# Attention, FFN and expert layers on one core: whole-array tail and B/C products, a masking in one pass, scales for each token tile apart, and a new order of the pieces

## The reference

```python
# sublayer 1: a chunked state-space mixer (64 heads of 8, state of 64)
B_mat = _rope_pairs(_rms_norm(B_mat) * B_norm_bias, cos, sin)     # 64 wide
C_mat = _rope_pairs(_rms_norm(C_mat) * C_norm_bias, cos, sin)
y = _ssd_chunked(x_gamma, A, B_mat, C_mat, dt) + _ssd_chunked(x_beta, A, B_shift, C_mat, dt)
# sublayer 2: a gated FFN, 704 hidden features, integer weights
gate = silu(x @ ((wq_gate - 128) * s_gate).T)
out = (gate * (x @ ((wq_up - 128) * s_up).T)) @ ((wq_down - 128) * s_down).T
# sublayer 3: attention by running sums, then a gated FFN of 1024
q, k, v = split(rms(x) @ w_qkv.T); q = rms(q); k = rms(k); w = exp(k)
y = sigmoid(q) * cumsum(w * v) / (cumsum(w) + 1e-6)
x = x + (u * silu(g)) @ w_out.T                       # u, g = split(y @ w_swiglu.T)
# sublayer 4: 16 experts of 448 hidden features, the best 4 of them for each token
```

## Time and profile before

| | us |
|---|---|
| median of 3 runs | 1955.8 (1946.88 to 1957.39) |
| the profiled execution | 1958.51 |
| its span, first to last instruction | 1956.7 |
| PE busy over the span | 1740.7 (89%) |
| DVE, POOL, ACT busy | 1320.4 (67%), 844.3 (43%), 751.6 (38%) |

### The profile page before, as it was taken

The page is one execution under the profiler, slowest core; times in us unless marked ns, Lnnn a source line. Parts: engine busy times, 40 slices in busy tenths (PEclk is TensorE's granted clock), DMA queues, the critical chain, the costliest instruction groups (busy, mean ns, idle before and its releaser), DMA issues. The chain is left out here.

```text
span 1956.7 us, 34760 instructions
## 1 busy us (share of the span) xinstructions
PE 1740.7 (89%) x8580; PEld 1208.8 (62%) x8581; DVE 1320.4 (67%) x3085; ACT 751.6 (38%) x1398; POOL 844.3 (43%) x791
## 2 busy tenths in 40 slices
PE   4699999999999999999999998863999999999980
PEld 2367667667677677676686675651655556665650
DVE  3788888888888888888889887321444444444435
ACT  3335445345345344454453452221322232332323
POOL 2033243333433433432533433123666667676654
PEclk7799999999999999999999999886999999999995
DMA  5523132142232231331321322636999999999997
GB/s 191 179 83 124 42 105 85 60 124 63 82 114 62 88 119 51 93 124 41 104 93 58 117 70 70 262 136 168 164 162 153 160 172 172 169 171 171 163 138 260
DMA packets 369673, 242.79 MB, mean 124 GB/s; under 512 B 250641, under 2 KB 348241, under 8 KB 369233
## 3 DMA queue, kind: packets, MB, share of 16 engines
q1 hardware_dynamic: 303824, 170.22, 32.6%
q0 software_dynamic: 40704, 67.40, 18.3%
q10 hardware_dynamic: 25088, 4.50, 1.2%
HBM read 121.33 MB, written 68.78 MB: 97 GB/s over the span
## 5 line engine op out<-in xcount | busy, mean ns | idle before, releaser
L1689 PE MATMUL pu<-w_all,xh 128*128 x1728 | 364.4, 357 | 56.1 <-DMA xh<-xin 40.6
L1689 PEld LDWEIGHTS pu<-w_all,xh 128*128 128x128 bf16 x1728 | 168.6, 99 | 209.3 <-issue 91.8
L1820 POOL DMA_INDIRECT sums_dram<-yo,meta_in x144 | 229.1, 1591 | 135.3 <-issue 70.9
L1772 DVE TENSOR_TENSOR hid<-pu,gate 128x448 f32<-128x448 f32 x144 | 90.0, 625 | 253.3 <-PE pu L1689 138.5
L838 PE MATMUL pb<-x1T,w_sw 128*128 128x256 f32 x1024 | 234.6, 384 | 0.7 <-ACT x1T L956 0.7
L838 PEld LDWEIGHTS pb<-x1T,w_sw 128*128 128x128 f32 x1024 | 193.3, 191 | 53.7 <-issue 14.9
L1704 PE MATMUL py<-w_all,hh 128*128 x1584 | 197.8, 274 | 3.0 <-DMA hh<-hs 3.0
L1704 PEld LDWEIGHTS py<-w_all,hh 128*128 128x128 bf16 x1584 | 155.7, 98 | 45.0 <-issue 4.2
L652 PE MATMUL pa<-w_in,xT 128*128 128x512 f32 (+1 forms) x384 | 159.8, 562 | 23.5 <-DVE masked L1272 14.2
L1807 POOL DMA_INDIRECT xin<-x_dram,meta_in x144 | 142.3, 988 | 67.7 <-issue 46.9
L1102 POOL DMA_INDIRECT xgs<-xg_dram,chosen_rows x112 | 122.1, 1091 | 93.0 <-DMA xg_dram<-xg 47.7
(11 more groups left out here) (244 smaller groups left out, 3118.4 us busy)
## 6 DMA issues: line engine op xcount, KB each, us to landing
w_stage<-in_w_ug SPq DMA_DIRECT2D x64, 224.0 KB
split_ug<-w_parts SPq DMA_DIRECT2D x64, 224.0 KB
w_all<-split_ug SPq DMA_DIRECT2D x16, 896.0 KB, 8.9
xg_dram<-xg SPq DMA_DIRECT2D x16, 512.0 KB, 2.8
w_stage<-in_w_dn SPq DMA_DIRECT2D x32, 256.0 KB
split_dn<-w_parts SPq DMA_DIRECT2D x32, 256.0 KB
w_all<-split_dn SPq DMA_DIRECT2D x16, 512.0 KB, 10.1
rows<-sums_dram SPq DMA_DIRECT2D x32, 256.0 KB, 5.3
```

Of the source, the lines that this page charges most:

```text
L1689: last = mm(pu[:, 2 * b + w, 0:EH], xh[:, m % XS, DC * xp + c, :], w_ug[:, bass.ds(e, 1), wp, c, w * EH:(w + 1) * EH], start=n == 0, stop= ...
L1820: nc.gpsimd.indirect_dma_start(out=sums_dram[m % 2], out_offset=bass.IndirectOffsetOnAxis(ap=meta[:, m, 0:1], axis=0), in_=yo[:, m % XS, : ...
```

## The change

- The 64 last gate columns and the 64 last up columns stand side by side in one weight (`w_gu`), so B1.5 is one product with 128 output rows (gate in rows 0 to 63, up in 64 to 127). ACT writes silu of the gate into partitions 64 to 127; the product with up goes into a tile of its own, `h_tail`, whose first 64 rows are zero, as are those of the last slice of `w_down`. B2.t then runs over 128 rows.
- `bcr` gets a third slot, with zeros ahead of B and C: the transposes of A3 are 128 wide, and A3L's products run over 128 rows, of which half are zeros or are multiplied by zeros.
- Masking: ACT copies the first tile's product to `cb_own`, DVE writes the second tile's over it under one mask, and one masked copy then fills `masked` for all levels.
- POOL makes the q/k scales for each token tile apart, ACT follows with that tile's k and q exponentials; B4.0 waits for the third of the four exponentials.
- `nothing` is half as wide and stored twice over by a repeated read; `sq_b` is gone (the squares are written into `yc`).
- Two pieces are cut in two (C7H from C7L, G1B from G1 on DVE), and the order of pieces is new on PE, ACT, POOL and DVE.

```diff
@@ ORDER
-    "PE": ("C7 A2 C7L F3.0 F3.1 B1T C8 A2L B1.0 B1.1 A3 B1.2 B1.3 B1.4 A3L B1.5 B2.0 B2.1 G1+ A4.0 B3T A4.1 B3.0 B3.1 "
-            "A4.2 B3V A4.3 A4.4 B4.0 B4.1 G2.0+ G2.1+ B5T A4.5 B5.0 B5.1 B5.2 A4.6 ...
+    "PE": ("C7 A2 C7L F3.0 F3.1 B1T A2L B1.0 C8 B1.1 A3 B1.2 B1.3 B1.4 A3L B1.5 B2.0 B2.1 A4.0 A4.1 G1+ B3T A4.2 B3.0 "
+            "B3.1 B3V A4.3 B4.0 G2.0+ B4.1 A4.4 G2.1+ B5T A4.5 B5.0 B5.1 A4.6 B5.2 ...
-    "ACT": ("A2 C7 WH.0 C7L A2S F3 B1T C8 A2L B1.0 B1.1 WH.1 A3 B1.2 B1.3 B1.4 A3L B1.5 G1+ B3T G2+ WH.2 B3 B3L B5T B5.0 "
-            "B5.1 G4+ B5.2 WH.3 WH.4 B5.3 B5.4 G3+ B5.5 B5.6 A5 B5.7 WH.5 A5L"),
-    "POOL": ("C7 A6- A2 AX.0 A2L AX.1 B2 B3 D8+ G1+ A5 B6"),
+    "ACT": ("A2 WH.0 C7 C7L A2S F3 WH.1 B1T C8 A2L B1.0 B1.1 B1.2 A3 WH.2 B1.3 B1.4 A3L B1.5 G1+ B3T WH.3 G2+ B3.0 B3.1 "
+            "B3L.0 B3L.1 G3+ B5T B5.0 B5.1 B5.2 B5.3 B5.4 B5.5 B5.6 WH.4 A5 B5.7 A5L WH.5 G4+"),
+    "POOL": ("C7 A6- A2 AX.0 AX.1 A2L B2 B3.0 B3.1 D8+ G1+ A5 B6"),
@@ PE: b1, b2, a3, b4
-                for w, weight in enumerate((w_gate, w_up)):
+                for w, first in enumerate((j * P, FM + j * P) if j < FJ - 1 else (2 * FM,)):
                     for c in range(DC):
-                        last = mm(pb[0:rows, 1 + j % 2, w * T:(w + 1) * T], weight[:, c, j * P:j * P + rows],
+                        last = mm(pb[:, 1 + j % 2, w * T:(w + 1) * T], w_gu[:, c, first:first + P],
...
-                    last = mm(pb[:, 3, t * D:(t + 1) * D], hT[0:rows, j, t * P:(t + 1) * P], w_down[0:rows, j, :],
-                              start=j == 0, stop=j == FJ - 1)
+                    h = hT[:, j, t * P:(t + 1) * P] if j < FJ - 1 else h_tail[:, t * P:(t + 1) * P]
+                    last = mm(pb[:, 3, t * D:(t + 1) * D], h, w_down[:, j, :], start=j == 0, stop=j == FJ - 1)
...
-                        last = nc.tensor.transpose(pa[0:N, 3, (2 * t + m) * P:(2 * t + m + 1) * P],
-                                                   bcr[:, t, m, :], ident)
+                        last = nc.tensor.transpose(pa[:, 3, (2 * t + m) * P:(2 * t + m + 1) * P],
+                                                   bcr[:, t, m:m + 2, :].rearrange("p z n -> p (z n)"), ident)
...
-                    pe.wait_ge(kq_exp.sem, kq_exp.at(s))
+                    pe.wait_ge(kq_exp.sem, kq_exp.at(s, 2 * NT - 1))
@@ DVE: a3_late
-                for t in range(NT):
-                    vec.copy_predicated(masked[:, :, :], halves[:, t, :, :], spread(pa[:, 2, t * P:(t + 1) * P], 1, LV)
-                                        ).then_inc(masked_ready.sem, 1)
...
+                vec.copy_predicated(cb_own[:, :], halves[:, LV, :], pa[:, 2, P:2 * P]).then_inc(masked_ready.sem, 1)
+                dve.wait_ge(masked_ready.sem, masked_ready.at(s, 1))
+                carrier.take()
+                vec.copy_predicated(masked[:, :, :], halves[:, 0:LV, :], spread(cb_own[:, :], 1, LV)
+                                    ).then_inc(masked_ready.sem, 1)
@@ POOL: b3, ACT: b3_late
+                pool.wait_ge(qk_ss_ready.sem, qk_ss_ready.at(s, 2 * (t + 1)))
+                root_mean(pb_, qk_ss[:, t, :], D, RMS_EPS).then_inc(qk_rms_ready.sem, 1)
...
+                act.wait_ge(qk_rms_ready.sem, qk_rms_ready.at(s, t + 1))
+                act_f(wv[:, t, 0, :], pb[:, 1 + t, D:2 * D], ACT.Exp, scale=qk_ss[:, t, 1:2]).then_inc(kq_exp.sem, 1)
+                act_f(eq[:, t, :], pb[:, 1 + t, 0:D], ACT.Exp, scale=qk_ss[:, t, 0:1]).then_inc(kq_exp.sem, 1)
```

More of the change, by code:

```diff
@@ L37 @@
 FJ = (FH + P - 1) // P
+FT = FH - (FJ - 1) * P
+FM = FH - FT
 SH = 1024
@@ L398, in layers_block @@
         padding = sb("padding", [P, cap // P, 4], U32)
-        nothing = sb("nothing", [P, NT * D])
+        nothing = sb("nothing", [P, D])
         w_stage = sb("w_stage", [P, 2, EJ // 2 * D])
@@ L937, in a3_late @@
                 act.wait_ge(cb_ready.sem, cb_ready.at(s))
+                act_f(cb_own[:, :], pa[:, 2, 0:P], ACT.Copy).then_inc(cb_copied.sem, 1)
                 act_f(cb_cross[:, :], pa[:, 3, 0:P], ACT.Copy).then_inc(cb_copied.sem, 1)
@@ L961, in b1 @@
             def b1(s, j):
-                rows = min(P, FH - j * P)
+                rows, to = (P, 0) if j < FJ - 1 else (FT, P - FT)
                 act.wait_ge(ffn_projected.sem, ffn_projected.at(s, j + 1))
@@ L965, in b1 @@
                     act.wait_ge(ffn_h.sem, ffn_h.at(s, j - 1))
-                act_f(sg[0:rows, j % 2, :], pb[0:rows, 1 + j % 2, 0:T], ACT.Silu,
+                act_f(sg[to:to + rows, j % 2, :], pb[0:rows, 1 + j % 2, 0:T], ACT.Silu,
                       scale=s_gu[0:rows, 0, j:j + 1]).then_inc(ffn_silu.sem, 1)
@@ L1077, in b2, with b3 @@
                                             ).then_inc(norm2[1].sem, 1)
-            def b3(s):
-                pb_.start(s)
-                pool.wait_ge(qk_ss_ready.sem, qk_ss_ready.at(s))
-                root_mean(pb_, qk_ss[:, :, :].rearrange("p t m -> p (t m)"), D, RMS_EPS).then_inc(qk_rms_ready.sem, 1)
-                pb_.end()
+            def b3(s, t):
+                if t == 0:
+                    pb_.start(s)
+                pool.wait_ge(qk_ss_ready.sem, qk_ss_ready.at(s, 2 * (t + 1)))
+                root_mean(pb_, qk_ss[:, t, :], D, RMS_EPS).then_inc(qk_rms_ready.sem, 1)
+                if t == NT - 1:
+                    pb_.end()
             def a2(s):
@@ L1382, in b1 @@
             def b1(s, j):
-                rows = min(P, FH - j * P)
                 dve.wait_ge(ffn_silu.sem, ffn_silu.at(s, j + 1))
-                vec.scalar_tensor_tensor(hT[0:rows, j, :], pb[0:rows, 1 + j % 2, T:2 * T], s_gu[0:rows, 1, j:j + 1],
-                                         sg[0:rows, j % 2, :], ALU.mult, ALU.mult).then_inc(ffn_h.sem, 1)
+                a = P - FT
+                if j == FJ - 1:
+                    vec.scalar_tensor_tensor(h_tail[a:P, :], pb[a:P, 1 + j % 2, 0:T], s_gu[a:P, 1, j:j + 1],
+                                             sg[a:P, j % 2, :], ALU.mult, ALU.mult).then_inc(ffn_h.sem, 1)
+                    return
+                vec.scalar_tensor_tensor(hT[:, j, :], pb[:, 1 + j % 2, T:2 * T], s_gu[:, 1, j:j + 1],
+                                         sg[:, j % 2, :], ALU.mult, ALU.mult).then_inc(ffn_h.sem, 1)
             def b2(s):
@@ L1410, in b2_second, with b3 @@
                 normalised_twice(s, 0, x2, x2_ready)
-            def b3(s):
-                dve.wait_ge(v_projected.sem, v_projected.at(s))
-                for t in range(NT):
-                    dve.wait_ge(kq_exp.sem, kq_exp.at(s, t + 1))
-                    vec.tensor_tensor(wv[:, t, 1, :], wv[:, t, 0, :], pb[:, 3, t * D:(t + 1) * D], ALU.mult
-                                      ).then_inc(wv_ready.sem, 1)
+            def b3(s, t):
+                if t == 0:
+                    dve.wait_ge(v_projected.sem, v_projected.at(s))
+                dve.wait_ge(kq_exp.sem, kq_exp.at(s, 2 * t + 1))
+                vec.tensor_tensor(wv[:, t, 1, :], wv[:, t, 0, :], pb[:, 3, t * D:(t + 1) * D], ALU.mult
+                                  ).then_inc(wv_ready.sem, 1)
             def b4(s, part):
@@ L1962, in host_arrays @@
     pad = FJ * P - FH
-    s_gu = np.stack([np.pad(a(f"L0_ffn_s_{n}"), (0, pad)).reshape(FJ, P).T for n in ("gate", "up")], 1)
+    s_gate = np.pad(a("L0_ffn_s_gate"), (0, pad))
+    s_up = a("L0_ffn_s_up")
+    s_up = np.concatenate([s_up[:FM], np.zeros(pad, s_up.dtype), s_up[FM:]])
+    s_gu = np.stack([s_gate.reshape(FJ, P).T, s_up.reshape(FJ, P).T], 1)
+    gate, up = a("L0_ffn_wq_gate").T, a("L0_ffn_wq_up").T
     down = a("L1_ffn_W_down").transpose(0, 2, 1)
```

97 lines of the change are left out of this document (46 added, 51 removed), and 10 rows, old and new, of the table ORDER.

## The result

| | before | changed |
|---|---|---|
| median of 6 runs, us | 1955.19 (1946.88 to 1957.39) | 1948.48 (1944.29 to 1950.33) |
| the profiled execution, us | 1958.51 | 1946.5 |
| its span, us | 1956.7 | 1944.7 |
| one round of the steady part, us | 75.70 | 75.2 |

The ratio is 0.9959, with a 95% interval of 0.994 to 0.9978: 0.4% faster, where 1.2% was forecast. The time lies inside the range; the size is a third of what was promised. A round gained 0.5 us and not 1.5.

A forecast was written before the change was run, and what follows sets the result against it. PE was taken as the bound, DVE nearly as tight before x2n. Per round -0.56 us up to B3T and -0.96 behind it, -1.5, times 16 = -24.3 us from 1958.5, less 2.7 for the median: 1932 us, range 1905 to 1950.

The forecast's parts named there:

- PE's own work: PE, each round: B1.5 loses 4 of 8 records (-0.86 us), array size changes go (-1.40 us); together -2.26 us.
- PE up to the down product: PE before B2.0: nothing gained before B1.0, B1.2 waits 0.1 us; B2.0 starts at about 722.0 instead of 723.12.
- The large copy and y: DVE's large masked copy starts at about 722.05 and ends at 723.3; POOL's y wants to start at 722.7, during it.
- the bounds of the hold: DVE before x2n: y beside the copy holds u 0.9 us, y behind it 1.4 us; 1.1 us taken.
- rival B: y gets in ahead of the large copy; PE stops 1.5 us in the down product; 1944 us, chance 0.14.
- The sentence on the Trainium skill: Shared DVE/POOL port pair locked by whichever starts first: the large copy keeps y out, hold 1.4 us, sum 5 us worse.
- the second bound: y starts behind the large copy at 723.3 and ends at 725.3, so u on DVE is held 1.4 us.
- Behind B3T: Rest of the round after B3T: A4.1 moved ahead -0.86 us, B4.0 waits 0.3 more, B5T's 0.4 wait goes; -0.96 us.
- x2n: PE's wait for x2n ahead of B3T is the longest of its waits, 1.5 to 2 us a round.
- A: Rival: the y product costs nothing and PE's gain is kept; 1904 to 1914 us, chance 0.28.
- C: Rival: ACT's weight piece WH.3 waits for its late-issued load, delaying B4.0 by 2.7 us a round; 1975 us, chance 0.08.
- D: Rival: the new order is so tightly packed that small waits return the tail's gain; 1946 to 1965 us, chance 0.08.

The follow-up runs named there:

- experiment 11: The changed kernel with y first on POOL and, on DVE, the first hidden product ahead of the routing's position products: 1912.6 us, ratio 0.9793 to the kernel before.
- experiment 9: The changed kernel with only half of each selected row fetched, the other half staying zero: 1938.49 us, ratio 0.9929 to the kernel before.
- experiment 1: The changed kernel with y on POOL back between the 4th and 5th row selection: 1939.43 us, ratio 0.9908 to the kernel before.
- experiment 5: The changed kernel with y on POOL ahead of all seven row selections: 1919.31 us, ratio 0.9806 to the kernel before.

## Why the prediction was wrong

**PE's own work (-2.26 us): right.** B1.5 has 4 records, the four transposes take 559.23 - 558.79 = 0.44, A3L 565.09 - 564.42 = 0.67, and where nothing stops it (experiment 11) the first half of the down product takes 630.59 - 628.00 = 2.59 us, so 5.2 for both, as forecast, against 5.96. C8's move gained nothing, A2L waits 0.34 us for the silu of z.

**PE up to the down product: right where completions are on time.** Counted from C7, B2.0 was forecast at 20.17 us; it stands at 20.32 in experiment 11 and at 20.04 in experiment 9. In the changed kernel it is 21.18, with the late completions ahead of it, which no row of before announced.

**The large copy and y: both placed well, where completions are on time.** The copy was forecast 722.05 - 701.83 = 20.22 us after C7. In experiment 9, whose round begins at 542.74, it starts at 562.98, 20.24 us after. In the changed kernel it starts so in one round of 14 and in the typical one at 568.37 - 545.91 = 22.46, since its input is late. y was forecast at 20.87 and stands at 20.59 there and 20.58 in the changed kernel.

**The failed step is the bounds of the hold**: "y runs beside that copy and ends at 724.7, then u, due at 723.75, is held 0.9 us; or y starts behind it at 723.3 and ends at 725.3, then u is held 1.4 us". Both let the copy finish in its own time, because it starts first. Experiment 9 shows a third case, in 13 of 14 rounds: y starts 0.35 us behind the copy (up to 0.59), runs its full 1.97 us, and the copy takes 3.34 instead of 1.16, so it is held 2.2 us. The changed kernel itself shows a hold of the copy in three rounds; in the other 11 a second thing, which the prediction put at nothing, comes to the same: PE's completions are 1.9 to 2.75 us late, the copy starts 2.2 us late and ends at the same place behind y. Where they come from stays open. The tail's product stands behind the copy and PE's down product behind that. With the hold and the prediction's own numbers: copy until 722.05 + 1.22 + 2.2 = 725.5, tail's product until 725.9 where B2.0 wants it at 724.2, PE stops 1.7 us; then 3.83 us of DVE work, B2 at 729.8, B3T at 733.7. That is +0.5 - 0.96 = -0.46 us a round, and 1958.5 - 7.4 - 2.7 = 1948.4 us. The measured median is 1948.48. That close is luck in part: the parts measured are +0.34 and -0.82 a round, and most of the rounds got there by the late completions.

This is rival B's mechanism, including the stop inside the down product (1.5 us forecast; 1.8 in experiment 9). B was given 0.14 because it was tied to a wrong condition, that the selections end 0.65 us earlier. It needed no y ahead of the copy: in experiment 9 a y that starts 0.35 to 0.59 us behind it was enough.

The sentence on the Trainium skill (SBUF — State Buffer, "SBUF: two separate sides") would have led to the second bound, 5 us above the forecast, and by a mechanism that did not show: in it the copy keeps y out, while in experiment 9 y keeps the copy waiting. The page gives the shared port pair to whichever instruction starts first, for the whole of it. The hold until the other has ended agrees with the traces. Who is held differs from case to case. When POOL makes xg it has been idle; in the changed kernel a DVE product with two SBUF operands that began 0.25 us earlier ran in its own time, and xg took 2.20 us (2.00 in the kernel before), as the page says:

```profile
550.71 0.62 DVE L1520 TENSOR_TENSOR w_parts<-w_stage,w_parts 128x448 bf16<-128x448 f32 x1
550.96 2.20 POOL L1087 TENSOR_TENSOR xg<-xs,g 128x1024 f32<-128x1024 f32 x1 [1.93 <-DVE g L1237]
```

When y stood directly behind a row selection, the DVE instruction was the one held, though by its recorded start it was first: the copy by 0.35 to 0.59 us in experiment 9, the decay product by 0.24 in the round shown of experiment 1. Whatever that lead was, the copy ended 1.02 us after y, of the 1.16 it needs, so it had done next to nothing before y. By the recorded starts the page's "first" does not hold there; whether POOL had claimed the ports before its recorded start, no run shows.

**Behind B3T: -0.96 forecast, -0.82 measured.** B4.0 waits 0.33 us (0.3 forecast), B5T waits no more. What was left out is the wait of 0.29 to 0.30 us at the head of each round for x (L1381).

**x2n**: forecast as the longest wait, 1.5 to 2 us; it is 0.52, because PE loses its time earlier, in the down product. DVE's chain is later than forecast: it opens B2 at 27.78 us after C7 (573.69, L1399), where 728.7 - 701.83 = 26.87 was forecast.

**The other rivals.** A (y costs nothing) is experiment 5, not this change: it was priced at 1904 to 1914 us and gave 1919. C did not happen: ACT nowhere waits for a weight piece. D's mechanism did not show either, though the time fell into its band (1946 to 1965): the order is sound once y is out of its way.

## What to carry to other kernels

In these traces the POOL products of 128x1024 held DVE operations with two SBUF operands that they met until they had ended. Directly behind a row selection y held even one that had begun 0.2 to 0.6 us before it; xg, behind an idle POOL, didn't. So when an order is laid out, look at what stands beside each large POOL operation and at who waits behind that, and try it where POOL idles for another reason (in the kernel before the same move cost 0.9%): here that one entry took 1.5% off the changed kernel, where the whole change had taken 0.4%. And when PE gets faster next to an engine that is nearly as busy, price the two together: here the parts taken alone gave between 0.9% slower and 0.6% faster, all of them together 2.1%. And when two causes stand at one place, removing one of them and gaining nothing doesn't clear it: the other may be enough.

## What the runs showed of the hardware

In the changed kernel ACT saw the end of the B/C product late: its copy started 2.15 to 2.75 us after the modelled end in 10 of 14 rounds, 1.91 in one, 0.69 and 0.76 in two and 0.04 in one. The last hidden products before the down product are late in the same way, while PE's next instructions that wait for nothing started on time. Whether PE reports late or ACT is told late, the traces don't separate. The condition was not the seven selections (experiment 5 has them too); with half the bytes it was gone. The windows of 9 us around them, same columns as above, the last two being DMA share and GB/s, of the changed kernel and with half rows:

```profile
559.00:568.00 9.00, 8.03 (x42) 6.88 (x41) 5.10 (x15) 3.31 (x9) 7.46 (x7) 1.00 0.67 185
```

```profile
556.00:565.00 9.00, 9.00 (x46) 7.77 (x44) 7.26 (x15) 3.58 (x9) 7.45 (x7) 1.00 0.32 100
```

With half rows, at 0.32, they are late in no round; with y first the share is 0.49 in 547 to 556 us, and they are on time. But the share alone doesn't decide it: in 183 to 192 us of the changed kernel it is 0.67 as well (180 GB/s), and there they are on time (0.04 us). What connects the two stays open; that fewer bytes remove it is shown.

The hold between DVE and POOL also goes the other way, with DVE's instruction in its own time and POOL's longer: a row selection takes 0.94 us on POOL, and 1.45 where DVE's decay product (1.08 us, as alone) runs (562.53 in the changed kernel).

In one round (that of 696.36) the late completions let PE idle 2.45 us ahead of the down product, and right behind that idle the granted clock was 0.52 (1.2 GHz) for 3 us, with PE busy throughout:

```profile
719.20:722.30 3.10, 3.10 (x8) 2.52 (x9) 2.89 (x5) 0.18 (x1) 0.00 (x0) 0.52 0.00 1
```

That round took 773.62 - 696.36 = 77.26 us instead of 75.2. The kernel before, the changed one and seven others have one to four of 14 rounds that are 1.5 to 3 us longer than the rest; five have none. These rounds are part of every time given, so differences of a few us between medians, like that of experiment 9, can come from them alone.
